# Spreading the adjacency products of attention step two over quarters of a round, in a four-layer graph kernel on one Trainium2 core

## The reference

```python
def _adj_from_feats(Xa, W1, W2, W3):
    logits = (Xa @ W1) @ W2 @ (Xa @ W3).T
    # keep, row by row, the largest entries until their softmax mass reaches 0.9
    masked = jnp.where(keep, logits, -jnp.inf)
    return jax.nn.softmax(masked, axis=1)

S = S + jnp.eye(n)
Rf = S / S.sum(axis=1, keepdims=True)
Rb = S / S.sum(axis=0)[:, None]
Xf, Xb, Xa, Z = X, X, X, 0
for s in range(2):
    A = _adj_from_feats(Xa, W1, W2, W3)
    Xf, Xb, Xa = Rf @ Xf, Rb @ Xb, A @ Xa
    Z = Z + (Xf @ U1[s] + Xb @ U2[s] + Xa @ U3[s])
return layernorm(X + Z) * gamma + beta
```

## Time and profile before

| | |
|---|---|
| median of three runs | 3477.58 us (3473.49 to 3478.12) |
| the profiled execution, its own time | 3477.54 us |
| its span, first to last instruction | 3475.8 us |
| mean granted TensorE clock | 0.958 of full speed |
| TensorE busy | 3141.6 us, 90% of the span |
| TensorE weight loads | 2270.6 us, 65% |
| VectorE busy | 2449.9 us, 70% |
| ScalarE busy | 1598.2 us, 46% |
| GpSimd busy | 2154.7 us, 62% |

### The profile page before, as it was taken

How to read it: one execution, slowest core, us unless ns; L and a number is a source line. 1 busy time by engine, 2 the same in 40 slices (tenths; PEclk the granted TensorE clock), 3 DMA queues, 4 the chain that set the end, 5 groups by cost and what they waited for, 6 DMA issues and landing times. The chain is left out here.

```text
span 3475.8 us, 42043 instructions
## 1 busy us (share of the span) xinstructions
PE 3141.6 (90%) x13212; PEld 2270.6 (65%) x13212; DVE 2449.9 (70%) x3401; ACT 1598.2 (46%) x2357; POOL 2154.7 (62%) x4214
## 2 busy tenths in 40 slices
PE   4999989997799999999976689988899999996899
PEld 3888778885567777777754255544566666664788
DVE  6840123333998889888883799999988999998000
ACT  2311322225666666666653445545555555652100
POOL 2212421114788888888881677878988788886211
PEclk9999999998899999999988899999999999998899
DMA  7644344433112222122111111211222222233255
GB/s 254 241 146 145 116 151 167 165 130 87 44 54 59 61 63 60 57 60 64 57 37 58 47 56 53 57 48 51 58 82 75 78 80 82 74 87 99 96 197 173
DMA packets 140702, 327.59 MB, mean 94 GB/s; under 512 B 15456, under 2 KB 93664, under 8 KB 129248
## 3 DMA queue, kind: packets, MB, share of 16 engines
q1 hardware_dynamic: 140512, 325.30, 29.5%
HBM read 286.70 MB, written 38.54 MB: 94 GB/s over the span
## 5 line engine op out<-in xcount | busy, mean ns | idle before, releaser
L1025 ACT ACTIVATE junk<-E,negp 128x3327 uint8<-128x3327 f32 x208 | 637.3, 3064 | 141.3 <-issue 107.3
L1397 DVE SCALAR_TENSOR_TENSOR U<-E,trial 128x3327 f32<-128x3327 f32 x182 | 678.1, 3726 | 0.0
L920 PE MATMUL bank<-big,adj 128*128 128x512 f32 x1352 | 608.7, 601 | 8.7 <-ACT t L1051 8.7
L920 PEld LDWEIGHTS bank<-big,adj 128*128 128x128 f32 x1352 | 252.4, 192 | 328.9 <-issue 327.9
L297 PE MATMUL bank<-big,E 128*128 128x256 f32 x1664 | 366.7, 382 | 2.8 <-PEq L58 1.7
L880 PE MATMUL bank<-Hc,PT 128*128 128x256 f32 x1248 | 303.1, 395 | 65.5 <-ACT PT L1064 65.4
L880 PE MATMUL bank<-Hc,adj 128*128 128x256 f32 x1456 | 338.0, 384 | 16.4 <-ACT adj L1064 16.2
L297 PEld LDWEIGHTS bank<-big,E 128*128 128x128 f32 x1664 | 315.8, 191 | 50.3 <-issue 5.7
L1359 DVE TENSOR_REDUCE nmax<-E 128x1 f32<-128x3327 f32 x52 | 188.0, 3615 | 208.8 <-ACT E L1068 208.8
L880 PEld LDWEIGHTS bank<-Hc,adj 128*128 128x128 f32 x1456 | 279.5, 193 | 79.8 <-issue 22.5
L880 PEld LDWEIGHTS bank<-Hc,PT 128*128 128x128 f32 x1248 | 244.3, 198 | 126.3 <-ACT PT L1064 77.0
(11 more groups left out here) (248 smaller groups left out, 5750.2 us busy)
## 6 DMA issues: line engine op xcount, KB each, us to landing
adj<-adjT SPq DMA_DIRECT2D x131, 448.0 KB, 3.4
E<-adjT SPq DMA_DIRECT2D x32, 1664.0 KB, 6.9
adj<-adjT SPq DMA_DIRECT2D x104, 384.0 KB, 3.3
adj<-adjT SPq DMA_DIRECT2D x20, 1664.0 KB, 7.0
E<-adjT SPq DMA_DIRECT2D x26, 1216.0 KB, 5.8
xt<-xin SPq DMA_DIRECT2D x52, 128.0 KB, 5.8
x_d<-xn SPq DMA_DIRECT2D x52, 128.0 KB, 1.7
xt<-x_d SPq DMA_DIRECT2D x52, 128.0 KB, 5.3
```

The source lines that it names most:

```text
L920: last = mm(agg[:, 0:w], adj[:, SPAN * (k % 2) + j - AGG[k]], rhs[:, j], start=(j == 0), stop=False)
L1025: go(junk[:, 0:N], E[:, t % DEPTH, 0:N], func, bias=negp[:, t % 2, j:j + 1], scale=1.0, accum_out=acc_[:, t % 2, j:j + 1]).then_inc(summed ...
L1397: V_.scalar_tensor_tensor(out=U[:, 0:N], in0=e, scalar=point, in1=e, op0=ALU.is_ge, op1=ALU.mult, accum_out=found))
```

## The change

Three things.

1. The adjacency products of step two are placed quarter by quarter. A table gives how many quarters stand in each slot of each round. The first tile of step two has its four in round 27, one in each slot, in the step change. Rounds 33 and 34 have one tile each, all four quarters in the last slot, behind the last scores. Rounds 35 to 44 have five quarters, one of the first slots taking two. Rounds 45 to 58, which have the side pairs, have three, in slots 0 to 2. The last quarter of the last tile is in round 58 as before.
2. ScalarE's copy of a finished tile stands at the head of the slot after its last quarter, wherever that is (`freed`). GpSimd adds it in the next round (`sent`), so in rounds 39 and 43 it adds two tiles, in rounds 48, 52 and 56 none. SyncE's loads for `zin` move from slot 0 to slot 3 of the round in which a tile begins.
3. `KEEP_END` of step two goes from 0.75 to 0.85.

```diff
-KEEP_END = (0.8, 0.75)
+KEEP_END = (0.8, 0.85)
...
-LATE = 7
+CLOSE = 7
...
-            agg_at = lambda i: i if 0 <= i < NT else i - LATE if NT <= i - LATE < tiles else None
-            sent_at = lambda i: agg_at(i - 1)
+            sent_at = lambda i: i - 1 if 0 < i <= NT else None
+            split = {1: (1, 1, 1, 1), 7: (0, 0, 0, 4), 8: (0, 0, 0, 4)}
+            quarters, freed, begun, sent, m = {}, {}, {}, {}, SLOTS * NT
+            for i in range(NT + LAG + NT + 7):
+                if i < NT:
+                    quarters.update({(i, k): [SLOTS * i + k] for k in range(SLOTS)})
+                else:
+                    ahead = i - NT
+                    sizes = split.get(ahead, (1, 1, 1, 0) if 19 <= ahead <= 32 else (0, 0, 0, 0))
+                    if 9 <= ahead <= 18:
+                        twice = next(k for k in (1, 2, 3, 0) if (m + k) % SLOTS != SLOTS - 1)
+                        sizes = tuple(1 + (k == twice) for k in range(SLOTS))
+                    for k in range(SLOTS):
+                        quarters[i, k] = list(range(m, m + sizes[k]))
+                        for r in quarters[i, k]:
+                            if r % SLOTS == 0:
+                                begun.setdefault(i, []).append(r // SLOTS)
+                            if r % SLOTS == SLOTS - 1:
+                                freed[(i, k + 1) if k < SLOTS - 1 else (i + 1, 0)] = r // SLOTS
+                                sent.setdefault(i + 1, []).append(r // SLOTS)
+                        m += sizes[k]
...
-                                if n is not None:
-                                    sp.wait_ge(agg_part, SLOTS * n + k + 1)
-                                    if k < 2:
-                                        load_chunk(n, k + 2)
-                                    elif v is not None:
-                                        to = SPAN * (k - 2)
+                                for r in quarters[i, k]:
+                                    sp.wait_ge(agg_part, r + 1)
+                                    if v is not None and r >= last_quarter(i) - 1:
+                                        side, to = r - last_quarter(i) + 1, SPAN * (r % 2)
...
-                                    elif n + 1 < tiles:
-                                        load_chunk(n + 1, k - 2)
+                                    elif r + 2 < SLOTS * tiles:
+                                        load_chunk((r + 2) // SLOTS, (r + 2) % SLOTS)
...
-                                if k == 0 and second(n):
-                                    load_z(n)
+                                if k == SLOTS - 1:
+                                    for n in begun.get(i, ()):
+                                        load_z(n)
...
-                                if n is not None:
-                                    neighbours(n, k)
+                                for r in quarters[i, k]:
+                                    neighbours(r // SLOTS, r % SLOTS)
...
-                                if k == 0 and second(G):
-                                    act.wait_ge(agg_part, SLOTS * (G + 1))
-                                    if G >= 1:
-                                        act.wait_ge(z_step, G)
...
+                                if (i, k) in freed:
+                                    n = freed[i, k]
+                                    act.wait_ge(agg_part, SLOTS * (n + 1))
+                                    act.wait_ge(z_step, n)
...
-                            if second(G):
-                                b, q = G - NT, G % 2
-                                pool.wait_ge(agg_copied, G + 1)
+                            for a in sent.get(i, ()):
+                                b, q = a - NT, a % 2
+                                pool.wait_ge(agg_copied, a + 1)
```

More of the change, by code:

```diff
@@ L705, in build @@
             early = NT - LAG
-            spread = [b for i in range(rounds + 1) for b in [last_at(i)] if b is not None and i < tiles + LATE]
+            spread = [b for i in range(rounds + 1) for b in [last_at(i)] if b is not None and i < tiles + CLOSE]
             kept = len(spread)
@@ L1007, in _ @@
                                     for j in range(FIRST):
[L1008 removed]
+                                        last = mm(side_bank[k], adj[:, SPAN * ((last_quarter(i) - 1 + k) % 2) + j], soon[j], start=(j == 0), stop=(j == FIRST - 1))
                                     last.then_inc(side_done[k], 1)
```

27 lines of the change are left out of this document (15 added, 12 removed).

## The result

The changed kernel took 3513.04 us (median of three runs, 3509.74 to 3514.04) against 3477.58 before: ratio 1.0099, 95% interval 1.0086 to 1.0112. It is 35 us slower, where 22.5 us less were forecast. The profiled execution has a span of 3512.2 us (before 3475.8), 36.4 more. Lines of the code stand 22 further down around the change: L1345 of before is L1367 now.

What follows compares the result with a forecast made beforehand. The prediction took VectorE and TensorE to bound step two by turns, TensorE in rounds 45 to 57. Step change -3.5, rounds 35 to 44 +32, 45 to 57 -58, 58 and 59 +7: -22.5 us, 3455 us, range 3434 to 3476.

Steps and rivals of the forecast that it cites:

- All three signs: D (probabilities written) of round 44 much beyond 2500 us; three-quarter rounds still 52 us for two passes; passes not 74.
- the 5 us for the copies in rounds 39 and 43: Rounds 39 and 43: ScalarE's copy of the second tile waits for GpSimd's addition of the first, 5 us each.
- The step change: Up to D (probabilities written) of round 34: row maximum 5.4 us sooner, late start costs 1.5; net -3.5 to -4 us.
- the end of 7: Step change, up to round 34: the far end of the predicted gain, -7 us; the other end was +4.
- The two doubtful passes of round 44: Replay with KEEP_END 0.85 gave round 44 two more extraction passes, which slight noise could remove; together 18 us.
- the second line of the table: Rounds 35 to 44, five quarters: forecast 517 us against 485.6 before, +32 us.
- Rival 4: Slower: in rounds 39 and 43 ScalarE stands 19 us each for GpSimd's addition, waits double; 3504 us, chance 0.08.
- These are mostly rounds of three passes, whose length covers it: Other openings inside rounds 35 to 44, some 4 to 6 us where TensorE leads, are hidden by long three-pass rounds.
- TensorE 52.2 of 52.7: Round 46 before the change: TensorE's busy time in us, against VectorE's 41.0, read as TensorE bounding the round.
- 590: Rounds 45 to 57, three quarters: forecast length in us, against 648.1 before, -58, 18 of it two passes fewer.
- Two passes take 52 us because TensorE trails: Step two: where TensorE trails VectorE by over some 4 us, two-pass tiles take 52.0 us, about 2.5 more a round.
- a rival's condition: Rival 2: GpSimd and ScalarE clog rounds 35 to 44, VectorE and GpSimd excluding each other in SBUF; 3476 us, chance 0.16.

Runs made afterwards that it cites:

- cut quarter: Kernel before, with the last quarter cut from six adjacency products to one in rounds 45 to 57: 3471.7 us, ratio 0.9990.
- both mends: Changed kernel, with GpSimd adding early-finished tiles in the same round and ScalarE's tile copy moved ahead of its waits for GpSimd: 3469.55 us, ratio 0.9982.
- light sums: Kernel before, with GpSimd's seven sums and products over 256 columns cut to 16 in rounds 45 to 57: 3469.12 us, ratio 0.9980.
- both reliefs: Kernel before, with the last quarter cut to one product and GpSimd's seven wide instructions cut to 16 columns, rounds 45 to 57: 3444.7 us, ratio 0.9905.

## Why the prediction was wrong

All three signs that the prediction names as showing it wrong came: D of round 44 at 2504.5, 51.9 us for two passes in round 51, and 72 passes. Two steps failed: the 5 us for the copies in rounds 39 and 43, and above all the reading that TensorE's busy share makes it the bound of rounds 45 to 57.

**The step change: right in kind, too small.** TensorE in rounds 27 and 29 and VectorE in round 33 of the changed kernel, answering to the earlier trace rows:

```profile
1808.61 4.54 PE L902 MATMUL bank<-Hc,PT 128*128 128x256 f32 x12 [3.28 <-ACT PT L1086]
...
1853.95 1.09 PE L915 MATMUL tr<-ident,E 128*128 128x128 f32 x8
...
1921.82 3.62 DVE L1381 TENSOR_REDUCE nmax<-E 128x1 f32<-128x3327 f32 x1 [15.47 <-ACT E L1090]
```

The hole of 18.10 us fell to 3.28, and the turn of round 29 came 2.1 us later than before, where I had 3.9, and ran at the usual length (1.09 against 1.97). The row maximum came 7.1 us sooner, where my order of ScalarE gave 5.4, less 1.5 for the late start. D of round 34 moved 7.2 us and not 3.5, just past the end of 7 that I had given.

**Passes: the range right, the likely case not.** The two doubtful passes of round 44 did not come: 72, not 74. That hid part of the damage, and is the only reason why the second line of the table looks nearly right; by the counted passes the ten rounds should have taken 499 us and took 523.8. Of these 25 us, 13 are waits for scores: 2.6, 15.4, 2.7 and 13.6 us after rounds 35, 39, 41 and 43, where the prediction has 3, 7, 2 and 9. The other 12 are rounds longer than their price without such a wait: 52.1 and 51.9 us for the two passes of rounds 37 and 38, 43.6 and 44.0 for the one pass of rounds 39 and 43.

**Rounds 35 to 44: the term "5 us each" failed.** I put 5 us in rounds 39 and 43 for the copy that needs GpSimd's addition. It measured 13.85 and 12.11, and VectorE lost 15.4 and 13.6 behind it. I had taken GpSimd's 2189.83 from the earlier trace rows as fixed; with TensorE, ScalarE and so the norm later, x3 and the addition moved too, to 2195.1. Rival 4 named this mechanism, with 0.08: its 19 us for ScalarE's stand (18.6 in round 39) were nearer than my 5. "These are mostly rounds of three passes, whose length covers it" held: the openings inside rounds 42 and 38 waited 6.5 and 2.2 us, and VectorE had no wait for scores at the start of rounds 43 and 39.

**Rounds 45 to 57: the step that decides.** "TensorE 52.2 of 52.7" I took for the bound, and so counted 40 us from its relief. It was one bound of three. In the one-pass rounds GpSimd's ring lay 0.5 us behind it (48.8 against 49.3), in the two-pass rounds VectorE itself, and the cut quarter alone shortened the stretch by 1.5 us. The row stood there: GpSimd busy 46.43 of 52.7 in round 46, an engine in order whose result the next round's scores wait for. On top of it the new openings stood in these rounds (17.0 and 6.9 us in rounds 56 and 57).

The 54.5 us missing against 590 lie as follows in the changed kernel's trace. VectorE waits 41 us for scores, where I had some 3: 5.6, 5.8, 2.1 and 10.7 at the start of rounds 45 to 48, 6.4 in 54, 10.5 in 57. With both mends 31 of them are still there, so the openings account for some 10; the rest is left to the ring and to the 12 us or so by which TensorE enters round 45 behind, which no run tells apart. The other 16 us are in the rounds themselves: one-pass rounds without a wait took 41.6 to 43.0 and not 40.5, a two-pass round 51.9 and not 49.4.

TensorE's own price was right, 43.3 us forecast: two first turns of the changed kernel with no wait of TensorE between them are 42.7 us apart.

```profile
2567.04 1.04 PE L915 MATMUL tr<-ident,E 128*128 128x128 f32 x8
...
2609.74 1.04 PE L915 MATMUL tr<-ident,E 128*128 128x128 f32 x8
```

**"Two passes take 52 us because TensorE trails": wrong.** With the quarter cut, round 51 takes 51.8 and a round entered with a lag of 0.1 us 51.7; with light sums, 49.4 at a lag of 14 us. VectorE's own busy time falls from 49.94 to 47.31. It is GpSimd's wide sums that fall between VectorE's small instructions, and TensorE's lag has no part in it. Relieving TensorE by itself wins nothing of these 2.5 us a round: round 51 of the changed kernel took 51.9. In round 51 of the kernel before, five of VectorE's instructions that are under 1 us take 0.50 to 0.72 us and all of them together 12.2; with light sums none takes over 0.4, and together they take 10.1. In round 56 of the changed kernel, in which GpSimd adds no tile, none is long either (9.9 together), and its two passes took 49.0 us: there the change did win it.

**A slip in the sums.** With 49.4 us for a tile of two passes, as the prediction prices it, three come to 148 and four to 198; it has 151 and 202. Without the slip the forecast would have been 7 us lower still.

**Rounds 58, 59:** +7 forecast, +9.3 measured: with one pass more they took 100.0 us against 90.7.

What stays open: which instructions of GpSimd's chain have to move for the ring to open without leaving work out. Of the two norms each was moved alone; both together were not tried. Nor was VectorE's share of the light sums' gain measured apart from the ring's.

## What to carry to other kernels

Where one engine is busy 99% of a round, look for a second ring of the same length before pricing its relief: take the engine with the next highest share in that stretch and follow its chain to where it closes over the round. Two experiments alone and both together tell it apart; either alone looks like "no effect". Then look at the busy time of the engines that were not touched: a relief can speed up a third engine, as the light sums did with VectorE, and its gain is not the ring's. And an in-order engine's time of arrival must not be read off the old trace once the work ahead of it moves.

## What the runs showed of the hardware

A round of one pass has six VectorE passes over all columns with two operands in SBUF, and beside each one GpSimd instruction stretches to its full length. In round 47 of the cut kernel, VectorE and then GpSimd (three of the six; the others are L1346, L1302 and the last L1199 above, beside L1398, L1405 and L1445):

```profile
2579.70 3.68 DVE L1398 SCALAR_TENSOR_TENSOR U<-E,trial 128x3327 f32<-128x3327 f32 x1
...
2585.02 3.68 DVE L1398 SCALAR_TENSOR_TENSOR U<-E,trial 128x3327 f32<-128x3327 f32 x1
...
2590.29 3.68 DVE L1398 SCALAR_TENSOR_TENSOR U<-E,trial 128x3327 f32<-128x3327 f32 x1
...
2606.07 3.63 DVE L1419 MAX8 top<-U 128x8 f32<-128x3327 f32 x1 [0.24 <-DVE mass L1407]
...
2614.76 3.61 DVE L1445 SCALAR_TENSOR_TENSOR E<-U,E 128x3327 f32<-128x3327 f32 x1
...
2579.79 3.80 POOL L1249 TENSOR_SCALAR up<-up,cand,over 128x1 f32<-128x1 f32 x1
...
2585.12 3.63 POOL L1264 TENSOR_TENSOR parts<-cand,took 128x4 f32<-128x4 f32 x1
...
2590.37 3.68 POOL L1193 TENSOR_SCALAR negp<-cand 128x1 f32<-128x1 f32 x1
...
2606.73 0.73 POOL L1310 TENSOR_TENSOR xo<-xo,bet 128x256 f32<-128x256 f32 x1
...
2600.37 0.70 DVE L1402 COPY_PREDICATED ends<-side,trial 128x4 f32<-128x4 int32 x1
```

An instruction on one to four columns, 0.20 to 0.34 us elsewhere in the round, takes 3.6 to 3.8, and one on 256 columns 4.0 to 4.1 where others take 0.73; beside MAX8 a sum over 256 columns keeps its 0.73. Six times some 3.4 us is 20 of GpSimd's 43.4 us in the round, and light sums leave six such instructions in place, for then smaller ones are caught (3.2 to 3.8 us each in round 47 with both reliefs): 43.4 became 39.1.

The rows agree with the Trainium skill (SBUF — State Buffer, Who interferes with whom), by which a VectorE instruction with two SBUF inputs contends with a GpSimd instruction that reads SBUF, and one with at most one, outside the two-port modes, does not. I had used it as a rival's condition; it held for all six in this round.

The other way round, VectorE's L1402 on four columns takes 0.17 to 0.18 us in the first three evaluations of this round and 0.70 in the fourth (last row), beside GpSimd's sum over 256 columns from 2600.33 to 2601.06. Five instructions lengthened like this are most of the 2.5 us by which a tile of two passes takes 51.9 us and not 49.4.
